# Routed experts on one core: a third unit in flight, the quantiser two units later with its operands in PSUM

## The chip, the cores and the metric

The kernel runs on one core of a Trainium2 chip. The metric is device time in microseconds (us); a lower number is better. A core has five engines that work side by side and meet at semaphores: TensorE (PE, matrix products; PEld is its loading of weights), VectorE (DVE), ScalarE (ACT), GpSimd (POOL) and SyncE (SP, which only starts transfers here). Matrix products land in PSUM, eight banks of 2 KB per partition; everything else lies in SBUF.

## The reference, cut to what matters

Two layers over 16 sequences of 128 tokens with 256 features. Layer 0 is a grouped attention and then the block that is changed here, a routed feed-forward block; layer 1 is a latent attention and a feed-forward block whose weights are quantised in blocks of 32. What the changed stage computes:

```
logits = x @ classifier_w.T;  probs = softmax(logits)          # 8 experts + 4 that only pass x on
idx = top2(probs + bias);     w_full = 1.5 * probs at idx, else 0
for e in range(8):
    act_e = silu(x @ gate_w[e].T) * (x @ up_w[e].T)            # 256 -> 128
out = sum_e w_full[e] * (act_e @ down_w[e].T) + x * sum(w_full[8:])

# layer 1's weights, per block of 32 values:
scale = max(2 ** floor(log2(max |w|)) / 4, tiny);  v = w / scale
power = max(2 ** floor(log2 |v|), 1);  v = round(v / power * 2) / 2 * power
wq = clip(v, -6, 6) * scale
```

## The kernel before, in words

`routed_experts` takes the 16 sequences in 4 groups of 4 (512 tokens) and each group through 8 experts: 32 units. Unit `u` is expert `x = u % 8` of group `j = u // 8`. Each engine runs its own list of steps, `step(u, j, x)`: the first group written out, the other three as a loop (`Fori`), and three steps behind the last unit (`u` = 32 to 34) in which only what is left of the last units is done. Inside an engine the order is as written; an instruction that waits for a semaphore holds all behind it.

A unit runs through these instructions. TensorE: six products for the gate and six for up, each 512 columns wide (L871, a product of float32 accuracy is made of three), into two pairs of banks used in turn. ScalarE: `gated` = silu of the gate (L928). VectorE: `inner` = gated times up (L969). TensorE: select (L885), one product that spreads the route weights of this expert over 128 partitions into bank 6. VectorE: `h` = inner times that (L974). ScalarE copies `h` rounded (L937), GpSimd subtracts to get the rest (L1073); both parts are the operand of twelve down products of 256 columns (L894), which add up over the eight experts of a group in banks 4 and 5. After the last expert VectorE adds the sum to `x` (L988). GpSimd has scaled `x` before that for the experts that pass it on (L1058, L1061).

Before the change, in step `u`, TensorE issues gate and up of unit `u`, select of `u - 1`, down of `u - 2`; it waits ahead of the gate products for `inner` and `h` of unit `u - 2`. VectorE does `inner(u)`, `h(u - 1)`, and then its part of the quantiser.

The quantiser of layer 1's weights runs in the same units: one chunk of 384 columns takes two units. Even unit, VectorE: block maxima, their power of two, scale, its inverse (L1010, L1632, L1633, L1634, in `block_powers`); GpSimd multiplies by the inverse (L1079). Odd unit, VectorE: power of each element by a bit mask, at least 1 (L1019, L1020), plus a large multiple of it (L1021), minus the same (L1028), clipped to 6 (L1030), in `shift_up` and `shift_down`; GpSimd multiplies by the scale into bfloat16 (L1083). TensorE turns the chunk in three transposes in the next even unit (L906), ScalarE keeps it (L941). SP loads the chunks into two buffers. GpSimd also rotates the context for layer 1, one step per unit in the first five units of a group (`rotate_context`, L1105 to L1115).

At the start the routes must be known: VectorE makes them in 21 instructions while TensorE runs units 0 and 1. TensorE then turns the route weights, four transposes per group of sequences (L860, `routes(g)`), ScalarE and VectorE keep the two parts (L921, L960).

Of the kernel before, what the change touches and what calls it, by code (L numbers as in the profile page):

```python
# [19 lines left out]
U32 = mybir.dt.uint32  # L20
# [747 lines left out]
def routed_experts(nc, m, d):  # L768
# [7 lines left out]
    with ExitStack() as scope:  # L776
# [14 lines left out]
        power, shifted = sb("mx_power", [128, CHUNK]), sb("mx_shifted", [128, CHUNK])  # L791
# [4 lines left out]
        weight_ps, mx_ps = m.bank(6), m.ps16[:, 1, 0:CHUNK]  # L796
# [11 lines left out]
        mx_loaded = [sem(f"mx_loaded{i}") for i in range(2)]  # L808
        mx_step, mx_divided, mx_made, mx_turned, mx_kept = (
# [5 lines left out]
        weights_turned_ps = [m.bank(k)[0:WROWS, :] for k in (6, 7, 7, 7)]  # L815
# [35 lines left out]
        def _(pe):  # L851
            def routes(g):
                if g == 0:
                    pe.wait_ge(route, ROUTE_STEPS)
                if g == 2:
                    pe.wait_ge(w_lo, 2)
                if g == 3:
                    pe.wait_ge(mx_kept, 1)
                for s in range(4):
                    t = pe.transpose(weights_turned_ps[g][:, s * S:(s + 1) * S], weights[:, 4 * g + s, :], m.ident[:, :])  # L860
                t.then_inc(w_turned, 1)

            def step(u, j, x):
                par, old = x % 2, 1 - x % 2
                if inside(u, UNITS):
# [9 lines left out]
                if isinstance(u, int) and u == 1:  # L875
                    routes(0)
                    routes(1)
                    pe.wait_ge(w_lo, 1)
                    pe.wait_ge(m.selected, 1)
                if isinstance(u, int) and u in (2, 3):  # L880
                    routes(u)
                if inside(u - 1, UNITS):
                    if not inside(u, UNITS):
                        pe.wait_ge(h_made, u - 1)
                    pe.matmul(weight_ps, select[:, (x - 1) % EXPERTS, :],  # L885
                              weights_t[:, j if x else j - 1, :], start=True, stop=True).then_inc(weight_spread, 1)
                if inside(u - 2, UNITS):
                    expert = (x - 2) % EXPERTS
                    pe.wait_ge(h_lo, u - 1)
                    if expert == 0:  # L890
                        wait(pe, x_made, j)
                    for q, (ph, pw) in enumerate(PRODUCTS):
                        for s in range(4):
                            t = pe.matmul(down_ps[:, s, :], ht[par][:, ph, s * S:(s + 1) * S],  # L894
# [4 lines left out]
                if x % 2 == 0 and inside(u - 2, UNITS):  # L899
                    c = 4 * j + x // 2  # L900
                    pe.wait_ge(mx_made, c)
                    wait(pe, mx_kept, c - 1)
                    if isinstance(u, int) and u in (2, 4):
                        pe.wait_ge(w_lo, 2 + u // 2)
                    for i in range(3):
                        t = pe.transpose(mx_ps[:, i * 128:(i + 1) * 128],  # L906
                                         quantised[(x // 2 - 1) % 2][:, i * 128:(i + 1) * 128], m.ident16[:, :])
                    t.then_inc(mx_turned, 1)
# [8 lines left out]
        def _(act):  # L917
            def keep_weights(g):

                act.wait_ge(w_turned, g + 1)  # L920
                act.activation(weights_t[:, g, :], weights_turned_ps[g], ACT.Copy).then_inc(w_hi, 1)  # L921

            def step(u, j, x):
                par, old = x % 2, 1 - x % 2
                if inside(u, UNITS):
# [3 lines left out]
                if isinstance(u, int) and u == 1:  # L929
                    keep_weights(0)  # L930
                    keep_weights(1)
                if isinstance(u, int) and u in (2, 3):
                    keep_weights(u)
                if inside(u - 1, UNITS):
                    act.wait_ge(h_made, u)
                    wait(act, down_made, u - 2)
                    act.activation(ht[old][:, 0, :], h[old][:, :], ACT.Copy).then_inc(h_hi, 1)  # L937
                if x % 2 == 0 and inside(u - 2, UNITS):
                    c = 4 * j + x // 2
# [9 lines left out]
        def _(dve):  # L949
# [7 lines left out]
            def split_weights(g):  # L957

                dve.wait_ge(w_hi, g + 1)
                dve.tensor_tensor(weights_t[LO:2 * LO, g, :], weights_turned_ps[g][LO:2 * LO, :],  # L960
                                  weights_t[LO:2 * LO, g, :].bitcast(F32), ALU.subtract).then_inc(w_lo, 1)

            def step(u, j, x):
                par, old = x % 2, 1 - x % 2
                if inside(u, UNITS):
                    dve.wait_ge(gated_made, u + 1)
                    dve.wait_ge(up_made, u + 1)
                    wait(dve, h_made, u - 1)
                    dve.tensor_tensor(inner[par][:, :], gated[par][:, :], up_ps[par], ALU.mult).then_inc(inner_made, 1)  # L969
                if inside(u - 1, UNITS):  # L970
                    dve.wait_ge(weight_spread, u)
                    dve.wait_ge(inner_made, u)
                    wait(dve, h_lo, u - 2)
                    dve.tensor_tensor(h[old][:, :], inner[old][:, :], weight_ps, ALU.mult).then_inc(h_made, 1)  # L974
                if isinstance(u, int) and u == 0:
                    split_weights(0)
                    split_weights(1)
                if isinstance(u, int) and u in (2, 3):
                    split_weights(u)
                if inside(u, UNITS):  # L980
                    (shift_up if x % 2 else block_powers)(u, j, x)
                if x == 1 and inside(j - 1, GROUPS):
                    if not inside(j, GROUPS):
                        mean_and_variance(dve, m, parts_made, stats_made, range(B - 4))
                    dve.wait_ge(down_made, u - 1)
# [3 lines left out]
                if x % 2 and inside(u, UNITS):  # L989
                    shift_down(u, j, x)  # L990
                if x == 4 and inside(j, GROUPS) and inside(j - 1, GROUPS):
                    dve.wait_ge(x_made, j)
                    carry(dve, m)
                    for s in range(4):
                        dve.bn_stats(m.parts[:, 4 * (j - 1) + s, :], m.x[:, 4 * (j - 1) + s, :]).then_inc(parts_made, 1)
# [6 lines left out]
            def block_powers(u, j, x):  # L1002
# [7 lines left out]
                then(1, dve.tensor_reduce(scale[:, :], w.rearrange("p (n c) -> p n c", c=MX), AX.X, ALU.max,  # L1010
                                          apply_absolute_value=True))
                block_scale(dve, then, scale[:, :], inverse[:, :], 1.0)

            def shift_up(u, j, x):
# [4 lines left out]
                then(1, dve.tensor_scalar(power[:, :].bitcast(U32), w.bitcast(U32), EXPONENT, None, ALU.bitwise_and))  # L1019
                then(2, dve.tensor_scalar(power[:, :], power[:, :], 1.0, None, ALU.max))  # L1020
                then(3, dve.scalar_tensor_tensor(out=shifted[:, :], in0=power[:, :], scalar=ROUND, in1=w,  # L1021
                                                 op0=ALU.mult, op1=ALU.add))

            def shift_down(u, j, x):

                c, w = 4 * j + x // 2, raw[(x // 4) % 2][:, (x // 2) % 2, :]
                then = lambda k, instruction: mx_then(instruction, c, k, SCALE_STEPS)
# [1161 lines left out]
```

## Time and profile before

| what | value |
|---|---|
| median of 3 runs | 831.03 us (829.92 to 831.12) |
| the profiled execution's own time | 830.3 us |
| its span in the profile | 828.5 us |
| TensorE matmul busy | 754.8 us, 91% of the span |
| VectorE busy | 611.7 us, 74% |
| GpSimd busy | 571.5 us, 69% |
| ScalarE busy | 403.6 us, 49% |
| first and last gate or up product of the experts' stage | 171.44 and 335.8 us |

The profile is of one execution. Its time of 830.3 us holds the span and 1.8 us around it. Times of rows are counted from the span's start. Busy shares are means over stages with different limits, so a stage is read by its own windows and its timeline.

### The profile page before, as it was taken

Reading aid. Unit: us, or ns where it says so; the run is one execution under the profiler, and the core shown is the slowest. Engines: PE = TensorE matmul, PEld = TensorE weight load, DVE = VectorE, ACT = ScalarE, POOL = GpSimd, SP = SyncE. Lnnn points to the kernel's source line nnn. Section 1 sums busy time; section 2 is a strip of 40 time slices with the busy share of each in tenths; the row PEclk is TensorE's granted clock in tenths of the full one; section 3 lists DMA queues with packets and bytes.
Section 4 is the critical chain, followed back from the end, with each engine's and each line's share of the span. In section 5 each row is a group of like instructions: output and inputs, shape, how many; then the busy total and the mean of one; then the engine's idle time right before and its main releaser. Section 6 shows DMA issues by size and latency. Waiting matters only on the chain. (4 is left out here: it accounts for less than half of the span.)

```text
span 828.5 us, 14817 instructions
## 1 busy us (share of the span) xinstructions
PE 754.8 (91%) x4808; PEld 539.7 (65%) x4808; DVE 611.7 (74%) x1083; ACT 403.6 (49%) x1068; POOL 571.5 (69%) x590
## 2 busy tenths in 40 slices
PE   4999999869999999788999999999999999876786
PEld 2555555447878887666777777777777777652564
DVE  5898999867887878665656666776678675749994
ACT  1688888533223222216545454655455445454453
POOL 5667776336676757555656778788877887817996
PEclk9999999989999999989999999999999999998999
DMA  9200000040000010122110000000000000000001
GB/s 258 109 1 0 0 0 1 2 169 20 20 19 20 19 57 0 51 103 96 48 49 1 1 1 1 2 2 1 1 1 1 2 1 1 1 2 7 25 32 40
DMA packets 8763, 24.12 MB, mean 29 GB/s; under 512 B 1711, under 2 KB 5167, under 8 KB 8087
## 3 DMA queue, kind: packets, MB, share of 16 engines
q1 hardware_dynamic: 8154, 23.28, 8.5%
q8 instruction: 33, 0.54, 0.3%
q14 instruction: 27, 0.22, 0.1%
q10 hardware_dynamic: 549, 0.08, 0.1%
HBM read 21.26 MB, written 2.10 MB: 28 GB/s over the span
## 5 line engine op out<-in xcount | busy, mean ns | idle before, releaser
L1606 POOL TENSOR_TENSOR q<-turned 64x512 f32<-64x512 f32 x128 | 168.1, 1313 | 25.7 <-DVE turned L1532 9.5
L1283 PE MATMUL ps<-l_yt,a 128*128 128x512 f32 x576 | 145.6, 403 | 2.1 <-ACT p L1429 1.6
L1283 PEld LDWEIGHTS ps<-l_yt,a 128*128 128x128 f32 x576 | 106.2, 190 | 27.4 <-issue 4.7
L1593 POOL TENSOR_TENSOR p<-p,l_inverse 128x512 f32<-128x512 f32 x64 | 66.8, 1047 | 74.2 <-DVE l_inverse L1554 73.7
L1429 ACT ACTIVATE p<-ps,l_negmax 128x128 f32<-128x128 f32 x256 | 91.1, 382 | 43.2 <-DVE l_negmax L1523 43.2
L1532 DVE TENSOR_TENSOR turned<-ps,rope 128x1024 f32<-128x1024 f32 x64 | 78.1, 1220 | 44.5 <-PE ps L1283 41.9
L871 PE MATMUL ps<-yt_experts,wsplit 128*128 (+1 forms) x384 | 99.2, 409 | 5.7 <-DVE h L974 5.2
L467 DVE TENSOR_REDUCE negmax<-ps 128x4 f32<-128x512 f32 x128 | 84.3, 685 | 12.9 <-PE ps L290 12.3
L871 PEld LDWEIGHTS ps<-yt_experts,wsplit 128*128 128x128 f32 x384 | 72.4, 195 | 23.6 <-issue 5.4
L383 ACT ACTIVATE pt<-ps 128x512 f32<-128x512 f32 x128 | 71.0, 599 | 6.3 <-PE ps L312 4.0
L1523 DVE TENSOR_REDUCE l_negmax<-ps 128x4 f32<-128x512 f32 x64 | 41.2, 686 | 44.3 <-PE ps L1341 44.1
L1544 DVE TENSOR_TENSOR turned<-ps,rope 64x512 f32<-64x512 f32 (+1 forms) x96 | 65.5, 683 | 2.1 <-PE ps L1283 0.7
L1446 ACT ACTIVATE qs<-ps 128x512 f32<-128x512 f32 x32 | 19.1, 597 | 98.1 <-PE ps L1299 98.1
L1073 POOL TENSOR_TENSOR ht<-h,ht 128x512 fp32r<-128x512 f32 x32 | 44.7, 1398 | 27.5 <-ACT ht L937 27.1
L1323 PE MATMUL ps<-wc,cs 128*128 128x256 f32 x384 | 62.0, 298 | 1.4 <-DVE cs L1560 1.4
L290 PE MATMUL ps<-bd,qt 96*128 96x512 f32 x128 | 56.5, 483 | 4.2 <-DVE negmax L467 2.6
L937 ACT ACTIVATE ht<-h 128x512 fp32r<-128x512 f32 x32 | 20.2, 632 | 80.2 <-DVE h L974 77.9
L894 PE MATMUL ps<-wsplit,ht 128*128 128x256 f32 x384 | 52.9, 288 | 6.7 <-POOL ht L1073 5.4
L894 PEld LDWEIGHTS ps<-wsplit,ht 128*128 128x128 f32 x384 | 50.7, 195 | 11.6 <-POOL ht L1073 7.6
L1429 ACT ACTIVATION_READ_ACCUMULATOR p<-ps,l_negmax 128x1 f32 x256 | 56.9, 222 | 0.0
L1323 PEld LDWEIGHTS ps<-wc,cs 128*128 128x128 f32 x384 | 50.5, 192 | 1.7 <-DVE cs L1560 1.7
L312 PE MATMUL ps<-qt,bd 104*128 104x512 f32 x128 | 51.6, 429 | 0.0
(213 smaller groups left out, 1567.0 us busy)
## 6 DMA issues: line engine op xcount, KB each, us to landing
wide<-in_wide SPq DMA_DIRECT2D x8, 768.0 KB, 4.5
mx_raw<-in_mx SPq DMA_DIRECT2D x8, 384.0 KB, 3.1
x<-in_x SPq DMA_DIRECT2D x4, 512.0 KB, 8.9
ctx_t<-in_ctx_t SPq DMA_DIRECT2D x1, 2048.0 KB, 7.6
out<-x SPq DMA_DIRECT2D x16, 128.0 KB, 1.7
narrow<-in_narrow SPq DMA_DIRECT2D x8, 192.0 KB, 2.6
ktraw<-in_ctx_rows SPq DMA_DIRECT2D x1, 1248.0 KB
wraw<-in_gate SPq DMA_DIRECT2D x1, 1024.0 KB, 18.4
```

The costliest lines, as they stand in the source:

```text
L290: pe.matmul(scores[k % 2], qt[par][0:QROWS, half, g, :], bd[par][0:QROWS, half, :, :].rearrange("p k t -> p (k t)"), start=True, stop=True ...
L383: act.activation(pt[i][:, :], scores_t[i % 3], ACT.Exp, scale=scale).then_inc(exp_made, 1)
L467: dve.tensor_reduce(negmax[par][:, g, half * KV4:(half + 1) * KV4], scores[k % 2].rearrange("s (k t) -> s k t", k=KV4), AX.X, ALU.max, neg ...
L871: t = pe.matmul(out, w_at(pw, w + k * EXPERTS * INTER + x * INTER, INTER), run_of(m.yt[:, py, k, :, :], j).rearrange("p b s -> p (b s)"), ...
L894: t = pe.matmul(down_ps[:, s, :], ht[par][:, ph, s * S:(s + 1) * S], w_at(pw, 4 * FFN + expert * E, E), start=(expert == 0 and q == 0 and ...
L1283: out = pe.matmul(tile_bank(n, k), a[i][:, pa, kin, k * 128:(k + 1) * 128], yt[j % 2][:, py, kin, :, :].rearrange("p b s -> p (b s)"), sta ...
L1323: t = pe.matmul(proj_ps[:, half, s * E:(s + 1) * E], cs[n % 2][:, pc, (2 * half + s) * S:(2 * half + s + 1) * S], wc[:, pw, i, :], start=( ...
L1429: t = act.activation(p[:, head, s, :], scores_bank(n, head)[:, s * S:(s + 1) * S], ACT.Exp, bias=negmax[:, head, s:s + 1], accum_out=total ...
L1532: dve.tensor_tensor(turned[:, 2 * k:2 * k + 2, :].rearrange("p t (b s) -> p t b s", b=4), spread(tile_bank(n, k).rearrange("p (b s) -> p b ...
L1544: r = dve.tensor_tensor(turned[out_rows, k, :].rearrange("p (b s) -> p b s", b=4), tile_bank(n, 2)[in_rows, :].rearrange("p (b s) -> p b s ...
L1593: pool.tensor_tensor(p[:, head, :, :], p[:, head, :, :], spread(inverse[:, head, :], 2, S), ALU.mult).then_inc(normed[head], 1)
L1606: t = pool.tensor_tensor(out[rows[(head + half) % 2], head, :], turned[rows[head], half, :], turned[rows[head], 2 + half, :], ALU.add)
```

## The change

All of it is in `routed_experts`.

- TensorE: in step `u`, gate and up of unit `u`, select of `u - 2`, down of `u - 3`. Ahead of the gate products it waits for `inner(u - 2)` only; the wait for `h` stands before select.
- VectorE: in step `u`, `inner(u - 1)`, the quantiser's part for unit `u - 2` (`LEAD = 2`), then `h(u - 2)` (function `hidden`). In the first group's step 2 `h` stands before the quantiser.
- The addition to `x` moves from step 1 to step 2 of the next group, behind `h`; in odd steps it no longer stands inside the quantiser's part. The statistics of `x` (L995) move from four in step 4 to two in step 4 and two in step 6. GpSimd scales `x` in steps 6 and 7, not 3 and 7.
- The quantiser: `power`, the block maxima (`largest`) and a row of -6 (`lowest`) lie in PSUM bank 7, which only VectorE uses in these units. The clip's two constants become one constant and the operand `lowest`: `tensor_scalar` (L1030) becomes `scalar_tensor_tensor`.
- The transposed chunk moves from bank 7 to bank 6, which select also writes: the transposes wait for `h(u - 2)`, and select in odd units waits until ScalarE has kept the chunk.
- The turned route weights all use bank 6. Those of group 0 come in step 1 behind the products; those of groups 1 to 3 in steps 3, 4 and 5, between the gate and the up products.

The core of the diff (TensorE's steps first, then VectorE's):

```diff
-        power, shifted = sb("mx_power", [128, CHUNK]), sb("mx_shifted", [128, CHUNK])
+        shifted = sb("mx_shifted", [128, CHUNK])
...
-        weight_ps, mx_ps = m.bank(6), m.ps16[:, 1, 0:CHUNK]
+        weight_ps, mx_ps = m.bank(6), m.ps16[:, 0, 0:CHUNK]
+
+        NB = CHUNK // MX
+        power, largest = m.bank(7)[:, 0:CHUNK], m.bank(7)[:, CHUNK:CHUNK + NB]
+        lowest = m.bank(7)[:, CHUNK + MX:CHUNK + 2 * MX]
...
-                    wait(pe, h_made, u - 1)
...
+                        if first and u in (3, 4, 5) and made is up_made:
+                            routes(u - 2)
...
-                if inside(u - 1, UNITS):
-                    if not inside(u, UNITS):
-                        pe.wait_ge(h_made, u - 1)
...
                 if inside(u - 2, UNITS):
-                    expert = (x - 2) % EXPERTS
-                    pe.wait_ge(h_lo, u - 1)
...
+                    wait(pe, h_made, u - 2)
+                    if x % 2:
+                        wait(pe, mx_kept, 4 * j + x // 2 - 1)
+                    pe.matmul(weight_ps, select[:, (x - 2) % EXPERTS, :],
+                              weights_t[:, j if x >= 2 else j - 1, :], start=True, stop=True).then_inc(weight_spread, 1)
+                if inside(u - 3, UNITS):
+                    expert = (x - 3) % EXPERTS
...
-                if x % 2 == 0 and inside(u - 2, UNITS):
-                    c = 4 * j + x // 2
+                if x % 2 == 0 and inside(u - 2 - LEAD, UNITS):
+                    c = 4 * j + x // 2 - 1
...
-                    wait(pe, mx_kept, c - 1)
...
+                    pe.wait_ge(h_made, u - 1 if inside(u - 2, UNITS) else UNITS)
...
+                v, jv, xv = u - LEAD, j if x >= LEAD else j - 1, (x - LEAD) % EXPERTS
...
+                    dve.tensor_tensor(inner[old][:, :], gated[old][:, :], up_ps[old], ALU.mult).then_inc(inner_made, 1)
...
+                if inside(v, UNITS):
+                    (shift if x % 2 else block_powers)(v, jv, xv)
+                if x in (4, 6) and inside(j, GROUPS) and inside(j - 1, GROUPS):
+                    dve.wait_ge(x_made, j)
+                    carry(dve, m)
+                    for s in range(x - 4, x - 2):
+                        dve.bn_stats(m.parts[:, 4 * (j - 1) + s, :], m.x[:, 4 * (j - 1) + s, :]).then_inc(parts_made, 1)
+                if inside(u - 2, UNITS) and not (first and u == 2):
+                    hidden(u, par)
+                if x == 1 and not inside(j, GROUPS):
+                    mean_and_variance(dve, m, parts_made, stats_made, range(B - 4))
+                if x == 2 and inside(j - 1, GROUPS):
...
+            def hidden(u, par):
+
+                dve.wait_ge(weight_spread, u - 1)
+                dve.wait_ge(inner_made, u - 1)
+                wait(dve, h_lo, u - 3)
+                dve.tensor_tensor(h[par][:, :], inner[par][:, :], weight_ps, ALU.mult).then_inc(h_made, 1)
...
+                then(2, dve.tensor_scalar(largest.bitcast(U32), largest.bitcast(U32), EXPONENT, None, ALU.bitwise_and))
+                then(3, dve.tensor_scalar(scale[:, :], largest, 0.25, 2.0 ** -122, ALU.mult, ALU.max))
+                then(4, dve.reciprocal(inverse[:, :], scale[:, :]))
...
+                then(1, dve.tensor_scalar(power.bitcast(U32), w.bitcast(U32), EXPONENT, None, ALU.bitwise_and))
+                then(2, dve.tensor_scalar(power, power, 1.0, None, ALU.max))
...
+                then(4, dve.scalar_tensor_tensor(out=w, in0=power, scalar=-ROUND, in1=shifted[:, :],
...
-                then(5, dve.tensor_scalar(w, w, 6.0, -6.0, ALU.min, ALU.max))
+                blocks = w.rearrange("p (n c) -> p n c", c=MX)
+                then(5, dve.scalar_tensor_tensor(out=blocks, in0=blocks, scalar=6.0, in1=spread(lowest, 1, NB),
+                                                 op0=ALU.min, op1=ALU.max))
```

ScalarE copies `h(u - 2)` in step `u` (before: `u - 1`), GpSimd subtracts for unit `u - 3` (before: `u - 1`) and multiplies for the quantiser's unit `u - 2` (before: `u`).

## Rows read from the trace of the kernel before

**Rows 1.** Busy time of each engine from unit 4 to unit 31.

```profile
197.90:333.20 135.30, 128.85 (x720) 108.03 (x718) 110.42 (x196) 37.86 (x68) 93.04 (x84) 1.00 0.07 24
```

**Rows 2.** Timeline of TensorE: start, us, what, [idle before <- what ended it].

```profile
180.06 1.09 PE L860 MATMUL ps<-ident,r_weights 128*128 128x128 f32 x8 [1.29 <-DVE r_total L1040]
185.40 5.07 PE L871 MATMUL ps<-yt_experts,wsplit 128*128 128x512 f32 x12 [2.77 <-DVE h L974]
...
218.15 3.01 PE L871 MATMUL ps<-yt_experts,wsplit 128*128 x12
...
231.40 1.66 PE L894 MATMUL ps<-wsplit,ht 128*128 128x256 f32 x12 [0.71 <-DVE x L988]
...
233.77 2.99 PE L871 MATMUL ps<-yt_experts,wsplit 128*128 x12 [0.25 <-DVE h L974]
236.60 0.39 PE L885 MATMUL ps<-r_weights_t,r_select 128*128 x1
236.82 1.59 PE L894 MATMUL ps<-wsplit,ht 128*128 128x256 f32 x12
238.29 2.99 PE L871 MATMUL ps<-yt_experts,wsplit 128*128 x12
...
243.02 3.01 PE L871 MATMUL ps<-yt_experts,wsplit 128*128 x12
...
333.19 3.00 PE L871 MATMUL ps<-yt_experts,wsplit 128*128 x12
```

**Rows 3.** Groups by line, VectorE: busy us, mean ns, idle before.

```profile
L1028 DVE SCALAR_TENSOR_TENSOR mx_raw<-mx_power,mx_shifted 128x384 f32<-128x384 f32 x16 | 16.7, 1041 | 0.5
L1021 DVE SCALAR_TENSOR_TENSOR mx_shifted<-mx_power,mx_raw 128x384 f32<-128x384 f32 x16 | 14.5, 905 | 0.6
L1633 DVE TENSOR_SCALAR mx_scale<-mx_scale 128x12 f32<-128x12 f32 x16 | 11.5, 720 | 0.6
```

**Rows 4.** Single lines of VectorE: shortest, median, longest in ns.

```profile
L1633 DVE TENSOR_SCALAR mx_scale<-mx_scale x16: 172/174/1819, 183.5 to 333.7; 128x12 f32<-128x12 f32 x16
L1020 DVE TENSOR_SCALAR mx_power<-mx_power x16: 359/360/1335, 185.9 to 337.9; 128x384 f32<-128x384 f32 x16
L1028 DVE SCALAR_TENSOR_TENSOR mx_raw<-mx_power,mx_shifted x16: 551/1030/1534, 187.1 to 338.9; 128x384 f32<-128x384 f32 x16
L974 DVE TENSOR_TENSOR h<-inner,ps x32: 678/680/689, 184.6 to 341.1; 128x512 f32<-128x512 f32 x32
L1965 DVE SCALAR_TENSOR_TENSOR f_hc<-f_h,ps x15: 1221/1221/1222, 751.1 to 815.0; 128x1024 bf16<-128x1024 fp8e4 x15
```

**Rows 5.** Single lines of GpSimd and ScalarE, the same columns.

```profile
L1073 POOL TENSOR_TENSOR ht<-h,ht x32: 1262/1297/1678, 186.7 to 343.5; 128x512 fp32r<-128x512 f32 x32
L937 ACT ACTIVATE ht<-h x32: 629/632/637, 185.3 to 341.8; 128x512 fp32r<-128x512 f32 x32
L1083 POOL TENSOR_TENSOR mx_quantised<-mx_raw,mx_scale x16: 831/834/837, 189.1 to 340.8; 128x384 bf16<-128x384 f32 x16
L1113 POOL TENSOR_TENSOR ctx_t<-ctx_t,kvt_sin x4: 1288/1293/1301, 202.4 to 321.8; 128x512 f32 x3, 128x512 f32<-128x512 f32 x1
L1061 POOL TENSOR_TENSOR x<-x,r_offset x4: 1892/1892/1893, 222.0 to 341.6; - x3, 128x1024 f32<-128x1024 f32 x1
```

**Rows 6.** Timeline of VectorE, first and last of four in an even unit.

```profile
213.19 0.55 DVE L1010 TENSOR_REDUCE mx_scale<-mx_raw 128x12 f32<-128x384 f32 x1
...
214.18 0.23 DVE L1634 RECIPROCAL mx_inverse<-mx_scale 128x12 f32<-128x12 f32 x1
```

**Rows 7.** Timeline: the statistics, and the tail behind unit 31.

```profile
325.51 1.41 DVE L995 BATCH_NORM_STATS2 parts<-x  x4
...
340.01 2.90 PE L894 MATMUL ps<-wsplit,ht 128*128 128x256 f32 x12 [1.89 <-POOL ht L1073]
...
346.53 1.22 DVE L988 TENSOR_TENSOR x<-x,ps 128x1024 f32<-128x1024 f32 x1 [3.96 <-PE ps L894]
```

**Rows 8.** Stage windows: busy us (count) of PE, PEld, DVE, ACT, POOL, then PEclk.

```profile
184.00:186.00 2.00, 0.60 (x2) 0.53 (x3) 1.97 (x4) 0.63 (x1) 1.91 (x3) 0.50 0.00 0
```

More of the change, by code:

```diff
@@ L811, in routed_experts @@
         block = scope.enter_context(nc.Block())
-        weights_turned_ps = [m.bank(k)[0:WROWS, :] for k in (6, 7, 7, 7)]
+        weights_turned_ps = weight_ps[0:WROWS, :]
         def steps(engine, step):
@@ L854, in routes @@
                     pe.wait_ge(route, ROUTE_STEPS)
-                if g == 2:
-                    pe.wait_ge(w_lo, 2)
+                else:
+                    pe.wait_ge(h_made, g)
                 if g == 3:
@@ L928, in step @@
                     act.activation(gated[par][:, :], gate_ps[par], ACT.Silu).then_inc(gated_made, 1)
-                if isinstance(u, int) and u == 1:
+                if first and u == 1:
                     keep_weights(0)
[L931 to L939, printed above, removed]
+                if first and u in (3, 4, 5):
+                    keep_weights(u - 2)
+                if inside(u - 2, UNITS):
+                    act.wait_ge(h_made, u - 1)
+                    wait(act, down_made, u - 3)
+                    act.activation(ht[par][:, 0, :], h[par][:, :], ACT.Copy).then_inc(h_hi, 1)
+                if x % 2 == 0 and inside(u - 2 - LEAD, UNITS):
+                    c = 4 * j + x // 2 - 1
                     act.wait_ge(mx_turned, c)
@@ L975, in step @@
-                if isinstance(u, int) and u == 0:
-                    split_weights(0)
[L977 to L985, printed above, removed]
+                first = isinstance(u, int) and u < UNITS
@@ new lines, in step @@
+                v, jv, xv = u - LEAD, j if x >= LEAD else j - 1, (x - LEAD) % EXPERTS
+                if inside(u - 1, UNITS):
+                    dve.wait_ge(gated_made, u)
+                    dve.wait_ge(up_made, u)
+                    wait(dve, h_made, u - 3 + 1)
+                    dve.tensor_tensor(inner[old][:, :], gated[old][:, :], up_ps[old], ALU.mult).then_inc(inner_made, 1)
+                if first and u == 1:
+                    split_weights(0)
+                if first and u in (3, 4, 5):
+                    split_weights(u - 2)
@@ new lines, in step @@
+                if first and u == 2:
+                    hidden(u, par)
[6 more added lines that the diff above has]
+                        dve.bn_stats(m.parts[:, 4 * (j - 1) + s, :], m.x[:, 4 * (j - 1) + s, :]).then_inc(parts_made, 1)
@@ L1086, in step @@
                     rotate_context(pool, m, rotated, j, x)
-                if inside(u, UNITS) and x in (3, 7):
+                if inside(u, UNITS) and x in (6, 7):
                     scale_x(j, x)
```

77 lines of the change are left out of this document (30 added, 47 removed).

## The prediction

> **What bounds the kernel now.** I read the page first: TensorE is busy nearly all the way, so only its holes can pay. The stage table [rows 1] narrows that to the experts' stage: from the fifth unit's products to the last's TensorE works 128.85 of 135.30 us at full clock, VectorE 110.42, GpSimd 93.04. All three are near the length of the stage, none fills it; the reader should ask what the holes are, and the TensorE timeline [rows 2] answers. A unit without quantised transposes takes 238.29 − 233.77 = 4.52 us, one with them 243.02 − 238.29 = 4.73. These are back to back: select starts 2.83 us into the unit, the down products at 3.05. But from unit 8 (218.15) to unit 31 (333.19) the 23 units take 115.04 us, where 12 × 4.73 + 11 × 4.52 is 106.5: some 8 us of holes. The first eight units are worse: units 0 and 1 run, then unit 2 starts only at 185.40.
>
> What ended the holes is in the timeline's brackets [rows 2]: the down products at 231.40 wait for VectorE's addition to x, the gate products at 233.77 for VectorE's `h`. In VectorE's queue `inner(u)` and `h(u-1)` stand behind quantising instructions whose length varies: the group means [rows 3] are far above the minima [rows 4]. (720 − 172) × 16 + (905 − 551) × 16 + (1041 − 551) × 16 is 8.8 + 5.7 + 7.8 = 22.3 us for L1633, L1021 and L1028 alone, taking L1021's minimum as that of L1028, the same form. GpSimd's subtraction stretches too (1262 to 1678 ns) [rows 5]. So VectorE and GpSimd hold each other up, at random places.
>
> **The quantiser's operands.** Five instructions of the second half get an operand in PSUM. Three of them are `tensor_scalar` today, some 360 ns each where nothing hinders (L1020's minimum). The trace has no 384-element instruction of these forms with PSUM; below is 360 ns (L1020 unhindered), above L1028's hindered mean, 1041 [rows 3, 4]. L974 (512 elements, one operand in PSUM) takes 680, so a column costs about 1 ns, and 384 give 552; L1965, with its bound in PSUM, takes 1221 for 1024, the same line. I take 560. Both L974 and L1965 hold still (678 to 689; 1221 to 1222) beside a busy GpSimd, so I take them as unhindered. Five instructions with about 35 ns between them: 2.95 us, no more than the mean 3.28 now, but steady. The first half stays at the clean 214.41 − 213.19 = 1.22 us [rows 6], call it 1.3, and the wait of L1633 (548 ns on average) is gone. VectorE then needs, per two units, 2 × 1.22 for `inner` and `h` (one starts 0.6 after the other), 1.3 and 2.95: 6.7 of 9.25, plus some 2.6 per group for the addition (1.22) and the statistics (1.41) [rows 7]. It is no bound.
>
> A page of the Trainium skill, "SBUF — State Buffer", section "Who interferes with whom", gives the reason: VectorE and GpSimd share a port pair, and an instruction with two SBUF inputs, or a two-port one, is held; with one SBUF input outside the two-port modes it isn't. By that rule the PSUM operands end the waits; the trace agrees (L1965 steady, L1633 172 to 1819).
>
> Another page speaks against the change: "Perfetto Trace Analysis", section "Optimizing Scalar/DVE Operations", gives VectorE about 125 ns of access overhead on PSUM against 60 on SBUF. By it each of the five would cost 65 ns more, the second half 3.3 us, and the sum below some 1.5 us more. The rows show no such step: L974 lies on the line of the SBUF forms.
>
> **The order: units 8 to 31.** Offsets are from a unit's first gate product. `inner(u-2)` is done a unit before gate(u) asks for it, so the old wait of the gate products is gone. Select(u-2) starts at 2.83, ends at 3.23; `h(u-2)` runs 3.3 to 4.0; then VectorE takes `inner(u-1)` to 4.6. In an even unit the powers end at 1.3 and `h` waits for select; in an odd one the shift runs from −0.1 to 3.0 and still ends before select does. ScalarE's copy (0.63) ends at 4.7, GpSimd's subtraction (1.27) at 6.0 to 6.1, and the down products want it at 4.5 + 3.05 = 7.6: 1.5 us to spare. GpSimd's multiplication (0.83) and one rotary step (1.29) [rows 5] may stand before that subtraction: they end at 5.3, the subtraction at 6.6, still in time. The new waits cost nothing while this holds: transposes need `h` at 4.4 and have it at 4.0; the odd unit's select needs ScalarE's copy of the transposed chunk, made within 0.7 us, and stands 2.8 us later. SP fills two buffers, each four units before its chunks are wanted; its queue has nothing else here.
>
> Where the stall goes: the addition to x. In step 2 of a group the last expert's down products end at 4.7; the addition takes 1.22 [rows 7] and ends 1.2 into step 3; `inner` 1.9, shift 4.8, `h` 5.5. GpSimd then has the multiplication (to 5.8) and a rotary step (to 7.1) before the subtraction, which ends at 8.4 against 7.6: 0.8 us, in three groups 2.4 us. After step 4 VectorE has caught up (the statistics, now two and two, lie in even steps with 2 us to spare). With 0.3 for the loop's turns: 106.5 + 2.4 + 0.3 = 109.2, against 115.04: **5.8 us gained**.
>
> **Units 0 to 8.** Routes end on VectorE at 180.0 [rows 2]. Now: `inner(0)` to 180.9, gate(2) from 180.95, not 185.40. The slow row of unit 2 (5.07 for 12, at granted clock 0.50 [rows 8], 1.2 GHz) followed nearly 3 us of idle TensorE; now 1.3 us idle precede it, so I take 3.0. Then select(0) at 183.8, `h(0)` 184.9, powers 186.2, GpSimd's division and rotary step 188.4, its subtraction 189.7. Unit 3 runs 184.05 to 187.5 with four route transposes inside (half of the eight in 1.09 at 180.06, 0.6), its select at 187.6 after copy and split of the weights; the down products wait to 189.75. Unit 4 starts at 191.2; routes inside, select 194.75, down to 196.4; unit 5 at 197.0, unit 6 at 202.2; there `h(3)` (204.0, late by the third split and shift) holds the down products to 206.3; unit 7 at 208.0, unit 8 at 212.5. Against 218.15: **5.6 us gained**; 4.2 if gate(2) still runs at half clock.
>
> **The tail.** Before, from unit 31's start to the end of the last addition: 347.75 − 333.19 = 14.56 [rows 2, 7]. Now one more unit is open and the quantiser trails by two. From unit 31 (0): `h(29)` 3.9, down(29) 5.9 to 7.4 after its subtraction, `h(30)` after the powers 7.0; the last shift 7.0 to 9.9, `h(31)` 10.6, mean and variance to 11.5; subtraction 12.7, down(31) at 12.75, addition 1.22. That is 15.6 with down products of 1.6 us; at half clock, as the 2.90 of [rows 7], 16.9. Over 2 us of idle precede it, so I take 16.9: **2.3 us lost**. GpSimd's power for the reciprocal deviation ends just before. The stages behind start earlier and are unchanged.
>
> **Sum.** 5.8 + 5.6 − 2.3 = 9.1 us. The profiled execution took 830.3 (span 828.5 and 1.8 around it), so 821.2; the median of the runs shown, 831.03, stands 0.7 above it: **822.0 us**.
>
> **The rivals.** (a) *GpSimd's subtraction becomes the wait.* The spare is 1.0 us behind a rotary step; behind an x scaling (1.89, L1061) [rows 5] 0.5. Gaps between instructions on VectorE and GpSimd could eat it in odd units; 0.3 each over 16 is 5 us, giving 827. For it: one queue carries five kinds of work; against: it is steady once VectorE no longer holds it. Chance 0.20. (b) *The shared bank takes the gain.* Transposes and select use one bank, so TensorE's queue stops for `h` in even units, with gate products behind it. If `h` came at 5.0 instead of 4.0, 16 × 0.57 us would be all the gain: about 831. The powers would have to end at 4.3 rather than 1.3. Chance 0.06. (c) *Slower: PSUM operands don't free VectorE.* If the five instructions still wait as L1028 does (1.04 on average, up to 1.53), the shift takes 5.4 us; the spare of 1.5 plus 0.3 goes at 4.75, each odd unit stalls 0.65, 16 × 0.65 = 10.4, and the tail's shift adds 2.4: 822.0 + 12.8 = 834.8. It ends over 0.2% slower from 1.02 us an instruction on. L974 and L1965 speak against it. Chance 0.08. (d) *More than forecast:* both clocks full, no stall at the addition: 5.8 + 2.4 + 5.6 − 1.0 = 12.8, giving 818. Chance 0.06.
>
> **How the numbers follow.** The forecast holds 0.60, its own range 818.5 to 825.5 (below: both clocks full, or the low end of the PSUM price, 360 ns, by which a shift of 1.95 us spares the addition's 2.4 us and 1.0 in the tail; above: gate(2) at half clock and the stall at the addition twice as long). The range 818 to 827 takes in it, most of (a), and half of (d). A measurement here can tell 0.2% (1.7 us) from no change; (a), (d) and the forecast are faster: 0.86; (b) 0.06; (c) 0.08.
>
> **What would show it.** L1633, L1021 and L1028 with minima equal to maxima, 0.55 to 0.6 us for all five; gate products without a bracket naming `h`; units of 4.52 and 4.73 save near step 4 of groups 1 to 3; unit 2 starting near 181 with products of 3.0 us; the last addition 16 to 17 us after unit 31's start. The prediction is wrong if the down products wait for GpSimd in most odd units, or if VectorE's PSUM instructions vary as L1028 does now.

## The result, and the profile after

| kernel | median us | range, runs | ratio to before (95% interval) |
|---|---|---|---|
| before | 831.08 | 829.92 to 836.04, 4 | 1 |
| after | 818.62 | 818.42 to 820.66, 4 | 0.9852 [0.9824, 0.9881] |

Faster by 1.5%, or some 12 us; the forecast was 822.0 us in 818.0 to 827.0, so the median lies at the low end of it. The profiled execution took 820.66 us with a span of 818.8, against 828.5: 9.7 us.

**The stage.** Windows of after: start to unit 8, units 8 to 31, tail, and the last stage of the kernel. Columns as in [rows 8].

```profile
171.00:213.50 42.50, 38.11 (x189) 30.71 (x189) 31.01 (x68) 12.80 (x22) 20.90 (x23) 0.92 0.26 92
213.50:321.30 107.80, 105.05 (x612) 91.08 (x612) 82.05 (x171) 33.58 (x58) 76.38 (x73) 1.00 0.08 26
321.30:339.00 17.70, 13.22 (x74) 11.45 (x74) 11.64 (x33) 4.00 (x8) 11.89 (x10) 0.81 0.00 0
...
660.00:814.00 154.00, 128.81 (x889) 86.73 (x888) 116.79 (x173) 75.15 (x181) 115.54 (x84) 0.94 0.04 12
```

TensorE is now idle for 2.75 of the 107.80 us between unit 8 and unit 31. Its timeline in after, which answers [rows 2] and [rows 7]:

```profile
171.22 7.34 PE L879 MATMUL ps<-yt_experts,wsplit 128*128 128x512 f32 x24
179.85 0.66 PE L866 MATMUL ps<-ident,r_weights 128*128 128x128 f32 x4 [1.29 <-DVE r_total L1050]
180.74 3.02 PE L879 MATMUL ps<-yt_experts,wsplit 128*128 128x512 f32 x12 [0.23 <-DVE inner L977]
...
189.46 2.93 PE L902 MATMUL ps<-wsplit,ht 128*128 128x256 f32 x12 [1.62 <-POOL ht L1086]
...
213.57 2.91 PE L879 MATMUL ps<-yt_experts,wsplit 128*128 x12
216.32 0.39 PE L893 MATMUL ps<-r_weights_t,r_select 128*128 x1
216.54 1.59 PE L902 MATMUL ps<-wsplit,ht 128*128 128x256 f32 x12
217.98 0.34 PE L912 MATMUL ps<-ident,mx_quantised 128*128 128x128 bf16 x3
218.13 3.01 PE L879 MATMUL ps<-yt_experts,wsplit 128*128 x12
...
222.63 2.91 PE L879 MATMUL ps<-yt_experts,wsplit 128*128 x12
...
231.70 2.91 PE L879 MATMUL ps<-yt_experts,wsplit 128*128 x12
...
235.74 1.68 PE L902 MATMUL ps<-wsplit,ht 128*128 128x256 f32 x12 [0.90 <-POOL ht L1086]
...
237.41 3.01 PE L879 MATMUL ps<-yt_experts,wsplit 128*128 x12
...
321.37 3.01 PE L879 MATMUL ps<-yt_experts,wsplit 128*128 x12
...
328.38 2.18 PE L902 MATMUL ps<-wsplit,ht 128*128 128x256 f32 x12 [2.11 <-POOL ht L1086]
...
331.58 0.76 PE L893 MATMUL ps<-r_weights_t,r_select 128*128 128x512 f32 x1 [0.67 <-ACT wq L947]
...
335.20 2.11 PE L902 MATMUL ps<-wsplit,ht 128*128 128x256 f32 x12 [0.29 <-POOL ht L1086]
```

No bracket names `h` or the addition to `x` any more in units 8 to 31. What is left there is the row at 235.74 and its two repeats, at 273.18 and 310.63 (0.92 each); a unit with such a row takes 237.41 − 231.70 = 5.71 us instead of 218.13 − 213.57 = 4.56. The last addition to `x` starts at 337.35 and takes 1.22, so the stage ends at 338.57, against 347.75: 9.2 us earlier.

Single lines of VectorE and GpSimd in after (shortest, median, longest in ns), against [rows 4] and [rows 5]:

```profile
L1023 DVE TENSOR_SCALAR ps<-ps x16: 178/178/179, 185.2 to 326.7; 128x12 uint32<-128x12 uint32 x16
L1033 DVE TENSOR_SCALAR ps<-ps x16: 566/566/567, 187.9 to 329.8; 128x384 f32<-128x384 f32 x16
L1034 DVE SCALAR_TENSOR_TENSOR mx_shifted<-ps,mx_raw x16: 557/557/558, 188.5 to 330.4; 128x384 f32<-128x384 f32 x16
L1036 DVE SCALAR_TENSOR_TENSOR mx_raw<-ps,mx_shifted x16: 557/557/558, 189.1 to 330.9; 128x384 f32<-128x384 f32 x16
L1086 POOL TENSOR_TENSOR ht<-h,ht x32: 1262/1292/1302, 188.1 to 333.9; 128x512 fp32r<-128x512 f32 x32
```

In these lines of VectorE minimum and maximum are 1 ns apart. L1033 was the 360 ns L1020 and takes 206 ns more with its operands in PSUM; L1036 was L1028, at 551 to 1534. GpSimd's subtraction, up to 1678 before, is steady too.

What made the length vary before is seen where the two engines overlap. The first row of each pair is GpSimd's, the second the same instruction of VectorE, before as L1021, after as L1034:

```profile
228.16 1.29 POOL L1073 TENSOR_TENSOR ht<-h,ht 128x512 fp32r<-128x512 f32 x1 [0.17 <-POOL kvs L1107]
228.24 1.62 DVE L1021 SCALAR_TENSOR_TENSOR mx_shifted<-mx_power,mx_raw 128x384 f32<-128x384 f32 x1
```

```profile
237.68 1.30 POOL L1086 TENSOR_TENSOR ht<-h,ht 128x512 fp32r<-128x512 f32 x1
238.18 0.56 DVE L1034 SCALAR_TENSOR_TENSOR mx_shifted<-ps,mx_raw 128x384 f32<-128x384 f32 x1
```

Before, L1028 took 1.50 to 1.53 us in the eight chunks in which it overlapped a GpSimd instruction, and 0.55 to 0.56 in the other eight. So the waits before were not at random places.

### The profile page after: what moved, and what is told of

Same layout as the page of the kernel before. It is cut to its first block and busy times, and to the rows that moved or that the text cites. A ratio compares the mean times of both kernels' runs of the same rounds, so it can differ in the third digit from the quotient of the medians.

```text
span 818.8 us, 14824 instructions
## 1 busy us (share of the span) xinstructions
PE 751.6 (92%) x4808; PEld 539.1 (66%) x4808; DVE 597.1 (73%) x1087; ACT 404.4 (49%) x1068; POOL 567.7 (69%) x590
## 5 line engine op out<-in xcount | busy, mean ns | idle before, releaser
L879 PE MATMUL ps<-yt_experts,wsplit 128*128 (+1 forms) x384 | 97.2, 402 | 0.2 <-DVE inner L977 0.2
L902 PE MATMUL ps<-wsplit,ht 128*128 128x256 f32 x384 | 55.0, 296 | 7.6 <-POOL ht L1086 7.6
L902 PEld LDWEIGHTS ps<-wsplit,ht 128*128 128x128 f32 x384 | 52.9, 202 | 12.1 <-POOL ht L1086 10.2
L1086 POOL TENSOR_TENSOR ht<-h,ht 128x512 fp32r<-128x512 f32 x32 | 41.2, 1289 | 11.2 <-ACT ht L943 9.9
```

The source lines that it names most:

```text
L879: t = pe.matmul(out, w_at(pw, w + k * EXPERTS * INTER + x * INTER, INTER), run_of(m.yt[:, py, k, :, :], j).rearrange("p b s -> p (b s)"), ...
L902: t = pe.matmul(down_ps[:, s, :], ht[old][:, ph, s * S:(s + 1) * S], w_at(pw, 4 * FFN + expert * E, E), start=(expert == 0 and q == 0 and ...
```

## The experiments

The theory: VectorE's waits beside GpSimd end because of the PSUM operands, and the order turns this into time, since `inner` and `h` are ready before they are asked for. The rival: one of the two halves does all of it. A second question is the price of the extra unit in flight and of the trailing quantiser at both ends of the stage.

All ratios are to before on the same chip. "0 to 8" and "8 to 31" are from the first gate product of the one unit to that of the other in the profiled execution, "tail" is from unit 31 to the first product of the next stage.

| run | median us (range, runs) | ratio, interval | 0 to 8 | 8 to 31 | tail |
|---|---|---|---|---|---|
| before | | 1 | 46.71 | 115.04 | 14.89 |
| after | 818.62 | 0.9852 [0.9824, 0.9881] | 42.35 | 107.80 | 17.53 |
| after, again | 820.70 (818.41 to 821.45, 6) | 0.9858 [0.9827, 0.9890] | 42.01 | 107.84 | 16.78 |
| operands alone | 832.48 (830.02 to 834.82, 12) | 1.0007 [0.9986, 1.0027] | 52.33 | 110.35 | 14.55 |
| operands, loop | 828.41 (826.17 to 831.21, 12) | 0.9962 [0.9940, 0.9983] | 46.99 | 110.55 | 15.41 |
| order alone | 825.18 (821.56 to 828.25, 7) | 0.9912 [0.9877, 0.9947] | 41.79 | 108.33 | 19.48 |
| no lead | 826.83 (823.86 to 828.75, 10) | 0.9930 [0.9907, 0.9953] | 47.18 | 107.59 | 17.50 |
| rotary late | 818.03 (815.76 to 818.07, 5) | 0.9835 [0.9804, 0.9866] | 42.11 | 105.10 | 17.53 |
| rotary late, again | 816.33 (815.25 to 817.49, 6) | 0.9818 [0.9779, 0.9857] | 40.88 | 105.11 | 17.52 |
| rotary both | 816.66 (815.63 to 818.91, 6) | 0.9822 [0.9782, 0.9862] | 40.51 | 105.16 | 16.77 |
| tail short | 821.94 (819.32 to 822.20, 6) | 0.9874 [0.9845, 0.9904] | 42.12 | 107.85 | 15.56 |
| tail short, again | 819.55 (816.42 to 821.16, 6) | 0.9844 [0.9802, 0.9885] | 42.40 | 107.81 | 15.77 |
| all three | 817.21 (814.12 to 820.35, 6) | 0.9832 [0.9798, 0.9867] | 40.49 | 105.11 | 15.55 |

**After, again.** No edit.

> The changed kernel once more, unaltered. The profiled execution of it took 820.66 us at a mean granted clock of 0.979, the three others 818.4 to 818.7 at 0.985 to 0.987. Theory: the 2 us between them are TensorE's clock and nothing else, so every time here goes with its clock: 818 to 819 at 0.985 or above, 820 to 821 at 0.98. Rival: the profiler itself costs 2 us, so a profiled execution is slow at any clock.

The profiled execution was the fastest of the six (818.41), where in the first series it was the slowest of four (820.66): the profile itself does not make the difference. Its windows:

```profile
171.00:213.50 42.50, 36.75 (x195) 29.63 (x195) 30.88 (x68) 12.69 (x22) 20.81 (x23) 0.96 0.26 92
213.50:321.30 107.80, 105.03 (x611) 91.11 (x610) 81.98 (x171) 33.56 (x58) 76.59 (x73) 1.00 0.08 26
321.30:339.00 17.70, 11.48 (x81) 9.95 (x80) 12.37 (x35) 4.17 (x8) 11.89 (x10) 1.00 0.00 0
...
660.00:814.00 154.00, 127.70 (x899) 86.28 (x904) 117.17 (x173) 76.05 (x184) 115.99 (x84) 0.97 0.04 13
```

The middle is the same to 0.04 us. What differs is the granted clock, 1.00 against 0.81 in the tail and 0.97 against 0.94 in the last stage. So two executions of one kernel can lie 2 us apart, and below I compare stretches first, totals second. My theory, that every time goes with its mean clock, did not hold: three others of the six had 0.985 and took 819.69, 820.55 and 820.85 us, where the first series had 818.42 to 818.68 at 0.985. What else sets them is open.

**Operands alone, in the whole stage and in the loop only.** Before, with the quantiser's power, maxima and bound in PSUM and the transposed chunk in bank 6; the first version also had to move the route transposes of groups 1 to 3 into units 2 to 4, the second leaves group 0 as it was.

```diff
-        weight_ps, mx_ps = m.bank(6), m.ps16[:, 1, 0:CHUNK]
+        weight_ps, mx_ps = m.bank(6), m.ps16[:, 0, 0:CHUNK]
...
+        power, largest = m.bank(7)[:, 0:CHUNK], m.bank(7)[:, CHUNK:CHUNK + NB]
...
+                        if isinstance(u, int) and u in (2, 3, 4) and made is up_made:
+                            routes(u - 1)
```

> The kernel before with its old order (gate of unit u, select of u - 1, down of u - 2, quantiser in the same unit); only power, maxima and bound move to PSUM bank 7, the transposed chunk to bank 6, and the route weights of groups 1 to 3 into units 2 to 4. Theory (both parts are needed: steady VectorE instructions remove the random holes, the order removes the wait for h at the gate products and the late start of unit 2): the five quantising instructions hold at 0.55 to 0.57 us, unit 2 still starts near 185, units 8 to 31 take 108 to 112 us, in all 824 to 829 us. Rival 1 (the operands are the whole gain): 817 to 821. Rival 2 (the order is the whole gain): 829 to 833.

> The kernel before in its old order; group 0 unaltered (route weights, banks, quantiser in SBUF), and only in groups 1 to 3 the quantiser's power, maxima and bound in PSUM bank 7 and the transposed chunk in bank 6. So the start is that of before. Theory (operands and order both fill the holes of units 8 to 31, and either alone does most of it): units 8 to 31 take 109.5 to 111.5 us against 115.0, the tail changes by less than 1 us: 826 to 828 us. Rival 1 (operands alone are worth nothing, as the first run with them, which also moved the route weights, came out at 832.5): 830 to 832. Rival 2 (in the old order the shared bank costs what the operands give): 829 to 833, with gaps at the transposes that name h.

Units 8 to 31 gain 4.7 and 4.5 us of the 7.2. The first version loses 5.6 at the start, since in the old order select must wait for each set of route weights that was turned a few instructions before. TensorE in operands alone:

```profile
186.99 0.77 PE L890 MATMUL ps<-r_weights_t,r_select 128*128 128x512 f32 x1 [4.45 <-DVE r_weights_t L960]
...
195.43 0.50 PE L890 MATMUL ps<-r_weights_t,r_select 128*128 128x512 f32 x1 [1.66 <-DVE r_weights_t L960]
```

The three stretches of this first version add up to 0.6 us more than before, and its time shows no change; the second version is faster by 0.4%. Both keep one stall in each of groups 1 to 3, shown on VectorE and TensorE in operands, loop:

```profile
229.99 0.56 DVE L1042 SCALAR_TENSOR_TENSOR mx_shifted<-ps,mx_raw 128x384 f32<-128x384 f32 x1
230.71 1.22 DVE L1001 TENSOR_TENSOR x<-x,ps 128x1024 f32 x1 [0.17 <-DVE mx_shifted L1042]
231.85 0.55 DVE L1049 SCALAR_TENSOR_TENSOR mx_raw<-ps,mx_shifted 128x384 f32<-128x384 f32 x1
```

```profile
234.55 0.34 PE L919 MATMUL ps<-ident,mx_quantised 128*128 128x128 bf16 x3 [0.82 <-DVE h L987]
```

The addition stands inside the shift, `h` comes late, and as transposes and select share a bank now, the transposes wait. This is rival (b) in small: 3 × 0.82 us.

**Order alone.** After, with power, maxima and bound in SBUF again.

```diff
-        power, largest = m.bank(7)[:, 0:CHUNK], m.bank(7)[:, CHUNK:CHUNK + NB]
+        power, largest = sb("mx_power", [128, CHUNK])[:, :], sb("mx_largest", [128, NB])[:, :]
...
+                then(5, dve.tensor_scalar(w, w, 6.0, -6.0, ALU.min, ALU.max))
```

> The changed kernel with power, maxima and bound back in SBUF and the clip as a tensor_scalar again; the order, the shared bank and the lead stay. Theory (both parts): VectorE's quantising instructions vary again (L1034 and L1036 0.55 to 1.7 us), but the spare of 1.5 us in the order takes up most of it: unit 2 near 181, units 8 to 31 108 to 111 us, in all 820 to 825 us. Rival 1 (the operands are the whole gain): 829 to 833. Rival 2 (the order is the whole gain): 817 to 820.

Lines of VectorE in order alone:

```profile
L1023 DVE TENSOR_SCALAR mx_largest<-mx_largest x16: 173/752/1060, 186.5 to 328.3; 128x12 uint32<-128x12 uint32 x16
L1033 DVE TENSOR_SCALAR mx_power<-mx_power x16: 359/904/1420, 189.6 to 331.9; 128x384 f32<-128x384 f32 x16
L1034 DVE SCALAR_TENSOR_TENSOR mx_shifted<-mx_power,mx_raw x16: 557/559/1629, 190.9 to 332.3; 128x384 f32<-128x384 f32 x16
```

The waits are back, though not in L1036, the L1028 of before: it stays at 557 to 559 ns, and no GpSimd instruction overlaps it here. L1034 is long (1.50 to 1.63 us) in the four of its 16 chunks in which one does. And yet units 8 to 31 take only 0.5 us more than after. The order has slack for the waits: it alone gives 6.7 of the 7.2 us, the operands alone 4.5 to 4.7, so most of the holes are closed by either. What the operands add to the order lies elsewhere: the tail is 2.0 to 2.7 us longer without them. Of that 0.8 to 1.2 us is the clock of the last down products (2.93 us here, 2.11 and 1.70 in the two runs of after); whether the longer waits led to it is not shown. They also start 1.1 to 1.5 us later. So both halves of the theory hold, but not its "turns into": the order does not need the steady instructions between units 8 and 31. By medians the operands are worth 4.5 to 6.6 us on top of the order; the three stretches account for 1.9 to 3.0 of it (0.5 + 2.0 to 2.7, less 0.2 to 0.6 in units 0 to 8), and the rest is in stretches that the edit does not touch.

**No lead.** After, with the quantiser in its old units.

```diff
-        LEAD = 2
+        LEAD = 0
...
```

> The changed kernel with LEAD = 0: the quantiser works in the unit itself again, all else as changed. Theory: the quantiser's first powers stand ahead of inner(0) and wait for the first load, so unit 2 starts 3 to 5 us later, part of which a stall later in the first units hides; behind unit 31 no shift stands before the last h, so the tail is 2 to 3 us shorter; units 8 to 31 stay at 107 to 109 us. In all 818 to 822 us. Rival: the lead only lengthens the tail, and without it the kernel is faster, 815 to 817 us.

TensorE in this run:

```profile
184.60 5.27 PE L879 MATMUL ps<-yt_experts,wsplit 128*128 128x512 f32 x12 [4.17 <-DVE inner L977]
```

Here unit 2's gate products wait until the first quantiser work is over and then run at a granted clock of 0.51, the lower level of 1.2 GHz (5.27 us for the twelve). The lead is worth 4.8 us at the start (47.18 against 42.35). I had expected the tail to be 2 to 3 us shorter without it, and it is not (17.50 against 17.53). No later stall hid the 4.8 us, the tail gave nothing, and the whole took 826.8 where I had said 818 to 822. Yet equal tails do not show that the trailing quantiser costs nothing there. VectorE's `h(31)`, first in after, then in after, again behind the last quantising instruction:

```profile
332.44 0.69 DVE L1006 TENSOR_TENSOR h<-inner,ps 128x512 f32<-128x512 f32 x1 [0.35 <-PE ps L893]
```

```profile
331.70 0.55 DVE L1039 SCALAR_TENSOR_TENSOR mx_raw<-mx_raw,ps 128x384 f32<-128x384 f32 x1
332.29 0.69 DVE L1006 TENSOR_TENSOR h<-inner,ps 128x512 f32<-128x512 f32 x1
```

In after `h(31)` waits for select, behind transposes, chunk copy and down products of unit 29. In after, again, where the tail ran at full clock, select ended at 331.57 and the shift held `h(31)` for some 0.6 us more. The run without the lead has no shift there, but its down products of unit 29 took 2.93 us, against 1.70 in after, again, which hides a gain of that size. So by these rows the trailing quantiser costs the tail some 0.6 us at most, not the 2 to 3 that I had argued.

**Rotary late, and both.** After, with the rotary steps of groups 1 to 3 in units 0, 1, 2, 4, 5 of a group; in the second version those of group 0 in units 0, 1, 3, 4, 5 as well.

```diff
-                if inside(u, UNITS) and 0 < x < ROTARY_STEPS:
-                    pool.wait_ge(rotated, ROTARY_STEPS * j + x)
+                places = (0, 1, 2, 3, 4) if first_group(u) else (0, 1, 2, 4, 5)
+                k = places.index(x) if inside(u, UNITS) and x in places else None
+                if k:
+                    pool.wait_ge(rotated, ROTARY_STEPS * j + k)
...
```

> The changed kernel, with GpSimd's rotary steps of groups 1 to 3 in steps 0, 1, 2, 4 and 5 instead of 0 to 4, so that none stands between the quantiser's multiplication and the subtraction of h in step 3. Theory (the addition to x makes shift and multiplication late, and the rotary step behind them holds the subtraction): the three waits of 0.90 to 0.92 us at the down products of step 4 go down to 0 to 0.2 each, units 8 to 31 take 105 to 106 us, 2 to 2.7 us less in all. Rival (VectorE itself is late there, h and ScalarE's copy with it): the waits stay at 0.6 or more, under 1 us gained.

> The same kernel as the one with the later rotary of groups 1 to 3, once more, beside the next two on one chip. 818.0 us if its first median was no accident; units 8 to 31 in 105.1 us, with no wait of the down products.

> After with the rotary steps of groups 1 to 3 in units 0, 1, 2, 4, 5 of a group and those of group 0 in units 0, 1, 3, 4, 5; the tail's order as in after. If each rotary step ahead of a subtraction that is already late sets its stall: units 8 to 31 in 105.1 us as with the later rotary alone (107.8 with after), units 0 to 8 in 40.5 as with all three edits (42.0 to 42.4 with after), the next stage 17.5 after unit 31's start, and the whole 2.7 + 1.7 = 4.4 us below after, about 815. If the start gained only through the other edits: units 0 to 8 stay at 42 and the whole is that of the later rotary alone, 818.

GpSimd around the stall of 235.74, first in after, then in rotary late:

```profile
232.17 0.83 POOL L1097 TENSOR_TENSOR mx_quantised<-mx_raw,mx_scale 128x384 bf16<-128x384 f32 x1 [3.58 <-DVE mx_raw L1039]
232.97 1.29 POOL L1127 TENSOR_TENSOR ctx_t<-ctx_t,kvt_sin 128x512 f32 x1
234.41 1.27 POOL L1086 TENSOR_TENSOR ht<-h,ht 128x512 fp32r<-128x512 f32 x1 [0.16 <-POOL ctx_t L1127]
```

```profile
233.00 0.84 POOL L1101 TENSOR_TENSOR mx_quantised<-mx_raw,mx_scale 128x384 bf16<-128x384 f32 x1 [3.58 <-DVE mx_raw L1039]
234.31 1.29 POOL L1090 TENSOR_TENSOR ht<-h,ht 128x512 fp32r<-128x512 f32 x1 [0.47 <-ACT ht L943]
```

The rotary step (1.29 us) behind a late multiplication made the subtraction late; without it the subtraction waits for ScalarE's copy. Units 8 to 31 took 105.1 to 105.2 us in all four runs with this edit and 107.8 in the four without it that have lead and operands as after: 2.7 us for three stalls, of each of which 0.3 us stays. The edit of group 0 takes the wait at 189.46 from 1.62 to 0.22 us, but another of 0.80 becomes 1.45, and only 0.4 us is left (40.51 against 40.88). I had put it at 1.7, most of which was the clock: rotary late, again ran units 2 to 8 without a stretch at the lower level, after did not (below).

**Tail short, and all three.** After, with select of unit 31 ahead of the down products of unit 29 and of the transposes, `h(31)` and the mean and variance ahead of the last shift, and GpSimd's last subtraction ahead of its last multiplication; the second version has the rotary edits too.

```diff
+                if isinstance(u, int) and u == UNITS:
+                    pe.wait_ge(h_made, UNITS - 1)
+                    pe.matmul(weight_ps, select[:, EXPERTS - 1, :], weights_t[:, GROUPS - 1, :],
+                              start=True, stop=True).then_inc(weight_spread, 1)
...
+                last = isinstance(u, int) and u == UNITS + 1
+                if last:
+                    hidden(u, par)
+                    mean_and_variance(dve, m, parts_made, stats_made, range(B - 4))
```

> The changed kernel with another order behind the last unit only: the select product of unit 31 ahead of the down products of unit 29 and of the transposes that share its bank, h(31), its copy and mean and variance ahead of the last shift, and both last subtractions and the reciprocal deviation ahead of GpSimd's last multiplication. Theory (the tail is the chain that the shared bank and the queues make: transposes, chunk copy, select, h, copy, subtraction): from unit 31 to the end of the last addition 14 to 15.5 us instead of 15.3 to 17.2, 1.5 to 3 us gained in all. Rival (the last shift and multiplication, two units late by the lead, set the end whatever the order): the end moves by less than 0.7 us, now at ScalarE's last chunk copy.

> The same kernel as the one with the new order behind the last unit, once more. If its later time was the granted clock of the last stage by chance, the whole comes 1 to 2 us below after's 818.6 to 820.7, at 817 to 819, in executions whose last stage has the clock of after's fast ones (0.97 from 660 us on, where the first execution had 0.93). If the shorter tail itself leads to a lower clock in the stages behind, it stands at 821 to 822 again and the last stage's clock is 0.93 to 0.94 again.

> The changed kernel with the two edits of rotary_late and tail_short, and in group 0 the rotary steps in steps 0, 1, 3, 4 and 5, so that the first subtraction does not wait behind the one of step 2. Theory: the terms add: 2.4 (additions) + 2 (tail) + 1 to 2.5 (the first down products start near 188.4 instead of 189.5, perhaps at full clock), 813 to 816 us where the changed kernel takes 818.4 to 821.4. Rival (each wait that goes uncovers another): 817 to 820.

The last addition and what follows it, in the first run:

```profile
334.64 1.22 DVE L1011 TENSOR_TENSOR x<-x,ps 128x1024 f32<-128x1024 f32 x1 [1.02 <-PE ps L906]
...
336.74 0.49 ACT L957 ACTIVATE wq<-ps 128x384 bf16<-128x384 bf16 x1 [4.94 <-PE ps L918]
...
337.54 3.44 PE L1236 MATMUL ps<-wide 128*128 128x128 f32 x16 [0.83 <-PEq L776]
```

The addition ends 13.9 us after unit 31's start (321.98), against 17.2 and 16.45. Now ScalarE's copy of the last chunk ends the stage, and the next starts 1.0 to 2.0 us sooner. The time does not follow. From the next stage's first product to the end of the span it took 482.9 and 481.9 us in the two tail-short runs (480.8 with all three), 479.9 and 478.3 in after, 476.9 and 478.6 in rotary late, all with the same code. In the last stage, from 660 us on, the granted clock was 0.93 and 0.93 (0.94), against 0.94 and 0.97, and 0.97 and 0.95. But such times come without the shorter tail too: no lead and operands, loop, which don't have the new order behind the last unit, took 482.3 and 482.4 us there, at 0.93 and 0.94. So nothing here shows that the shorter tail leads to the lower clock; that it never does is not shown either, and the second tail-short run, with a median of 819.55, fell between its two forecasts. All three, forecast at 813 to 816, took 817.2.

The best versions are rotary late, rotary both and all three, at 816.3 to 818.0 us. Their intervals overlap with each other and with that of after; against after only the 2.7 us of the stage is shown.

## Why the prediction was right, point by point

- **The quantiser's operands: right.** 553 to 567 ns against 560, steady. By [rows 4] a `scalar_tensor_tensor` took 551 at its shortest in SBUF; it takes 557 here, and 557 at its shortest in order alone. The rule of the Trainium skill, "SBUF — State Buffer", section "Who interferes with whom", agrees: with at most one input in SBUF none of the five was held (553 to 567 ns), beside a GpSimd instruction or not. The other, "Perfetto Trace Analysis", section "Optimizing Scalar/DVE Operations", would have had 65 ns more per instruction for PSUM; the trace shows 0 to 6 for this form. The 200 ns of the `tensor_scalar` forms are more than that rule gives.
- **Units 8 to 31: mechanism right, two sizes off, 1.4 us too long** (109.2 against 107.80). The unit with transposes takes 4.56, not 4.73: the row that I took for back to back held a hole of its own, so the units sum to 11 × (222.63 − 213.57) + 4.56 = 104.2, not 106.5. The stalls behind the addition are where they were put and for the reason given, as the rotary runs show, but a unit with one is 1.15 to 1.18 us longer, 3.5 in all and not 2.4. The loop's turns are in what is left, 0.1, not 0.3.
- **Units 0 to 8: 4.4 gained against 5.6.** Unit 2 starts at 180.74 (predicted 180.95) with 3.02 us of products (3.0), and the first down products at 189.46 (189.75). The missed term: these took 2.93 us, at a granted clock of 0.50 (1.2 GHz) behind 1.62 us of waiting. From their start to unit 4's are 2.73 us, where I had 1.45 at full clock; that is the whole difference. The full clock of unit 2 was in part luck: TensorE was idle for 1.29 us before the route transposes, as I had taken it, because units 0 and 1 ran partly at the lower level (7.34 us, a mean granted clock of 0.78). In after, again they took 5.74 at full clock, 2.89 us of idle followed, and the half clock fell on unit 2 instead (4.12 us). In rotary late, again it fell on neither, and there the start is 40.88, a gain of 5.8.
- **The tail: 2.6 lost against 2.3, by two errors that nearly cancel.** Down of unit 29 came at 7.0 us, not 5.9: its subtraction stands behind GpSimd's x scaling (325.21 to 327.10, the subtraction from 327.07), which I had counted as a rival's price but not in the tail. The delay runs through to the last down products (13.8 against 12.75). These took 2.11 us at a granted clock of 0.77, not the 2.90 that I had taken from [rows 7]. A wait for ScalarE's copy in the shared bank (0.67) was not foreseen. The tail's idle time is the chain of the last units, as the tail-short runs show; the last shift, behind which I had put `h(31)`, held it in after, again and not in after.
- **The sum: 9.1 predicted for the stage, 9.2 measured,** and 0.5 from the stages behind. That it is so close is luck: the three terms were off by +1.4, −1.2 and −0.3 us, and the stage began 0.2 us sooner. The median lies 2.0 below the profiled execution, where I had added 0.7 for before; in after, again it lies 2.3 above it (820.70, 818.41). That is the spread between executions, of which the clock is a part.
- **The rivals.** (a) is the three stalls and two before unit 8 (1.62 at 189.46, 0.80 at 207.37), not every odd unit. (b) cost nothing between units 8 and 31; in the tail the shared bank cost 0.67 once. (c) fell. (d) did not come, though the median lies near its 818: the stalls and the half clock stayed, and the units were shorter instead.

## What to carry to other kernels

Two edits that close the same holes don't add up: cost each alone against the slack that the other leaves, and look for the rest of its worth where there is no slack, at the ends of a stage. In a queue that works in order, a filler placed ahead of a late operand costs its consumer up to its own time in every round (here 0.9 us of 1.3); move it behind, one unit later. Compare stretches between two fixed instructions before totals: units 8 to 31 repeat here to 0.06 us, where totals of one kernel differ by 3. Stretches with idle time in them do not: the clock moved the start by 1.5 us and the tail by 0.8.

## What the runs showed of the hardware that was not expected

- TensorE's clock varies between executions at the same place. The first down products wait 1.62 us in after and run at 0.50 (the row at 189.46); behind the same wait they ran at 1.00 in after, again, and in rotary late, again (one row of each, in this order). In after, again the half clock had come earlier, on unit 2. In rotary late, again, whose first group is that of after, the rows from unit 0 to these products are those of after to 0.03 us, and yet the clock differs.

```profile
191.05 1.70 PE L902 MATMUL ps<-wsplit,ht 128*128 128x256 f32 x12 [1.62 <-POOL ht L1086]
```

```profile
189.56 1.69 PE L902 MATMUL ps<-wsplit,ht 128*128 128x256 f32 x12 [1.63 <-POOL ht L1090]
```

- In order alone about 20 us more of VectorE's time, (888 − 566) + (818 − 557) + (658 − 178) + (430 − 170) + (664 − 556) = 1431 ns of longer means in each of 16 chunks less 200 ns for the clip and the maxima, cost TensorE 0.5 us between units 8 and 31, in which 12 of the 16 chunks fall.
